# A depthwise convolution of 15 matmuls a channel: three of them get 128 weight columns instead of 64, and the two halves of the input patches are requested together

## What is computed

```
def _L1_conv_ref(x, w_large, w_small, ...):      # x: (1, 384, 192, 192), w_large: 13x13, w_small: 3x3
    out = _bn(_dwconv(x, w_large, 6), g_l, b_l, m_l, v_l) \
        + _bn(_dwconv(x, w_small, 1), g_s, b_s, m_s, v_s) + _bn(x, g_i, b_i, m_i, v_i)
    return out
x = x + _L0_conv_ref(_gn(x), ...)                # layer 0
x = x + _L1_conv_ref(_gn(x), ...)                # layer 1
```

## Time and profile before

| | us |
|---|---|
| median of 3 runs | 2976.05 (2973.62 to 2976.38) |
| the profiled execution | 2976.38 |
| its span, first to last instruction | 2974.7 |
| PE busy in the span | 2670.8 (90%) |
| DVE busy | 2522.6 (85%) |
| ACT busy | 1481.1 (50%) |

### The profile page before, as it was taken

The page is one execution under the profiler, slowest core; times in us unless marked ns, Lnnn a source line. Parts: engine busy times, 40 slices in busy tenths (PEclk is TensorE's granted clock), DMA queues, the critical chain, the costliest instruction groups (busy, mean ns, idle before and its releaser), DMA issues. The chain is left out here.

```text
span 2974.7 us, 50705 instructions
## 1 busy us (share of the span) xinstructions
PE 2670.8 (90%) x17273; PEld 1812.0 (61%) x17273; DVE 2522.6 (85%) x3512; ACT 1481.1 (50%) x1921; POOL 73.9 (2%) x143
## 2 busy tenths in 40 slices
PE   0049999999999999999995999983999999999998
PEld 0036666666666666666663566652777777777776
DVE  7969999999999999999997898984877777777774
ACT  0033445555554554553232667673655555555553
POOL 0010000000000000000000000000000000000000
PEclk9999999999999999999997999995999999999999
DMA  8964112222322322321004999988999999999985
GB/s 333 416 204 144 49 56 93 85 87 84 103 77 93 103 77 87 100 81 48 17 1 152 333 349 346 343 291 177 251 263 261 261 262 261 261 262 260 262 249 169
DMA packets 349112, 546.95 MB, mean 184 GB/s; under 512 B 143392, under 2 KB 254752, under 8 KB 345888
## 3 DMA queue, kind: packets, MB, share of 16 engines
q1 hardware_dynamic: 317504, 436.49, 47.5%
q10 hardware_dynamic: 31456, 108.48, 11.8%
HBM read 364.47 MB, written 180.44 MB: 183 GB/s over the span
## 5 line engine op out<-in xcount | busy, mean ns | idle before, releaser
L781 PE MATMUL qk_qb<-qk_xhi,whi 128*128 128x384 f16 x2592 | 846.4, 327 | 21.0 <-DVE qk_xlo L677 14.3
L781 PE MATMUL qk_qb<-qk_xlo,whi 128*128 128x384 f16 x2592 | 846.2, 326 | 0.0
L781 PE MATMUL qk_qb<-qk_xhi,wlo 128*128 128x384 f16 x2592 | 846.2, 326 | 0.0
L698 DVE SCALAR_TENSOR_TENSOR qk_dw<-qk_pool,qk_wd,qk_dw 128x768 f32<-128x768 f32 (+2 forms) x864 | 836.9, 1009 | 0.1
L685 DVE TENSOR_REDUCE qk_pool<-qk_qb 128x192 f32<-128x768 f32 x432 | 411.9, 954 | 68.7 <-PE qk_qb L781 51.9
L1491 ACT ACTIVATE cv_res<-cv_cb,cv_cst 128x288 f32<-128x288 f32 x384 | 189.8, 502 | 381.5 <-PE cv_cb L1634 331.3
L1628 PE MATMUL cv_cb<-cv_hi,cv_toep 128*128 128x288 f16 x1536 | 346.6, 286 | 35.5 <-DVE cv_lo_last L1559 32.8
L781 PEld LDWEIGHTS qk_qb<-qk_xhi,whi 128*128 128x128 f16 x2592 | 254.0, 98 | 184.2 <-DVE qk_xlo L677 17.5
L781 PEld LDWEIGHTS qk_qb<-qk_xhi,wlo 128*128 128x128 f16 x2592 | 253.9, 98 | 168.4 <-issue 1.2
L1634 PE MATMUL cv_cb<-cv_hi_next,cv_toep 128*128 128x288 f16 x1536 | 356.3, 293 | 0.0
L781 PEld LDWEIGHTS qk_qb<-qk_xlo,whi 128*128 128x128 f16 x2592 | 254.0, 98 | 162.8 <-issue 1.0
(11 more groups left out here) (163 smaller groups left out, 3466.3 us busy)
## 6 DMA issues: line engine op xcount, KB each, us to landing
cv_toep<-toeplitz_scratch SPq DMA_DIRECT2D x384, 256.0 KB, 4.7
patch_scratch<-pr_turned SPq DMA_DIRECT2D x75, 832.0 KB, 9.6
st_x<-in_x SPq DMA_DIRECT2D x24, 2304.0 KB, 17.1
qk_xf<-in_x SPq DMA_DIRECT2D x72, 768.0 KB, 4.3
pr_xb<-in_x SPq DMA_DIRECT2D x24, 2304.0 KB, 10.1
out<-cv_rows ACTq DMA_DIRECT2D x72, 768.0 KB, 5.7
cv_raw<-patch_scratch SPq DMA_DIRECT2D x25, 1300.0 KB, 9.8
cv_raw<-patch_scratch ACTq DMA_DIRECT2D x23, 1300.0 KB, 9.5
```

The source lines that it names most:

```text
L698: V.scalar_tensor_tensor(acc, pool[:, o, r + y:r + y + n, x:x + PW], wd[:, o, k:k + 1], acc, ALU.mult, ALU.add).then_inc(taps_done, 1)
L781: ins = nc.tensor.matmul(qbank[s % NQB][:, h, 0:2 * W], w[:, b, o * P:(o + 1) * P], x[:, par, j // 2, b, at_row:at_row + 2 * W], start=n = ...
```

## The change

Three edits in one stage:
1. `late` gets a second block of 64 columns per channel that GpSimd fills with zeros once. The three matmuls of L1631 take all 128 columns and write all 128 PSUM partitions (zeros are added to the lower 64), with the same 276 moving columns. SP waits for the zeros before the first load of `late`.
2. ACT requests its half of `raw` after the bank copy of channel 0, ahead of `last_high`, instead of after that of channel 5.
3. SP requests its half at its c = 9 instead of c = 8, behind the weights of channel 8, which wait for channel 0 too.

```diff
-        late = sb("late", [P, GRP, ERUN], F16)
+        late = sb("late", [P, GRP, 2, ERUN], F16)
...
-                sp.dma_start(late[:, part_of(q), :],
+                sp.dma_start(late[:, part_of(q), 0, :],
...
-                    if c == GRP // 2 and (inner or g + 2 < NG):
+                    if c == NTOEP + 1 and (inner or g + 2 < NG):
                         address(sp, (g + 2) * (TI * GRP * TJ))
                         sp.wait_ge(edge_done, g * NPC + NPC)
                         start.load_half(sp, g + 2, par, 0)
                     if inner or g < NG:
                         load_taps(g, c)
+                        if at(g, 0) and c == 0:
+                            sp.wait_ge(late_zero, 1)
...
+        @block.gpsimd
+        def _(gp):
+            nc.gpsimd.memset(late[:, :, 1, :], 0.0).then_inc(late_zero, 1)
...
-                    if c == 0:
-                        last_high(g, NPC - 1)
-                    if c == GRP // 2 - 3 and (inner or g + 2 < NG):
+                    if c == 0 and (inner or g + 2 < NG):
                         address(act, (g + 2) * (TI * GRP * TJ))
                         act.wait_ge(edge_done, g * NPC + NPC)
                         start.load_half(act, g + 2, par, 1)
+                    if c == 0:
+                        last_high(g, NPC - 1)
...
-                few = late[:, c, :].rearrange("p (m v) -> p v m", v=2)
+                few = late[:, c].rearrange("p r (m v) -> p v (r m)", v=2)
-                upper = bank[0:HP, 0:NPIX].rearrange("p (j i) -> p j i", j=OJ)[:, :, 0:EI]
...
-                    nc.tensor.matmul(upper, few[:, part], x[:, c, :, 0:EI], start=False, stop=False, skip_group_check=True)
+                    nc.tensor.matmul(whole[:, :, 0:EI], few[:, part], x[:, c, :, 0:EI], start=False, stop=False, skip_group_check=True)
```

More of the change, by code:

```diff
@@ L1368, in stage_depthwise @@
         bbank = [ctx.enter_context(nc.psum_tensor(f"cv_bb{i}", [P, 512], F32)) for i in range(NBB)]
-        cst_in = sem("cst_in")
+        cst_in, late_zero = sem("cst_in"), sem("late_zero")
         toep_in = [sem(f"toep_in{i}") for i in range(NTOEP)]
```

## The result

| | before | after |
|---|---|---|
| median of 4 runs each | 2974.84 (2972.04 to 2976.38) | 2937.91 (2936.08 to 2945.84) |
| span of the profiled execution | 2974.7 | 2934.1 |
| ratio | | 0.988 [0.986, 0.990] |

The account below looks back on a forecast made before the run. PE alone was taken to pace the depthwise stage, with pauses around its 64-column matmuls. The sum 2976.4 - 96.0 + 8.4 + 4.5 = 2893.3, with the median 0.3 lower, gave 2893 us, range 2874 to 2912.

Parts of the forecast that it names:

- 128 columns: The three 64-column matmuls of each depthwise channel, widened: both pauses go, 0.25 us for each of 384 channels, -96.0 us.
- rival D: Pauses around the 64-wide matmuls stay, coming from the change of line or weight tile, not width: 2976 to 2981 us, chance 0.04.
- The zeros: One memset before the first load of `late`: at most 2.4 us, hidden before PE's first matmul, taken as 0.
- The pair: Both halves of `raw` requested together make channel 9's weights late: 0.4 us for 21 groups, +8.4 us (0 to 15.8).
- the bound of 0.75: Most that channel 9's weights could be late per group, if the group's first store takes its turn first: 0.75 us.
- Group 0: SP's half goes out only after DVE's last `norm`, so PE waits once at channel 9: +4.5 us (0 to 6.5).
- The clock: PE's clock might fall after a wait: within the 6.5 us upper bound at group 0's channel 9, no term of its own.
- rival E: Slower: both halves hold up channel 9 in every group, from 4.4 us a group on; 2990 us with 5, chance 0.03.
- DVE and ACT, fits: DVE's 28.62 us fit a 33.4 us group (86%); ACT's bank copy behind the store keeps 1.6 us of slack.
- Rival B: Both halves of `raw` overlap at 406 GB/s, 6.5 us instead of 13, nobody waits: 2880 or 2876 us, chance 0.24.
- Rival C: Transfers pace the depthwise stage: a group takes 34.3 us, saving only 3.0, total 2909 us, chance 0.13.

## Why the prediction was wrong

- **128 columns, -96.0: right in kind, 2.6 us too high.** A group without waits fell from 37.29 to 33.40 us, so 24 of them by 93.4 us; the lower bound was 95. The forecast took 0.25 us a channel and 1.8375 for what is left; 0.243 went. Two readings in it were loose: from the last L1628 to the second L1634 are five steps, not six, and 0.22 us is the idle time of a weight load, of which some 0.12 us reached the matmuls on each side (0.247 for both). The 64-wide kernel with the pair keeps its pauses and the widened one has none, so rival D is refuted.
- **The zeros, 0: right.** The memset took 1.80 us (2.4 estimated) and ended before PE's first matmul by 11 us.
- **The pair, +8.4 (0 to 15.8): the step that failed.** Its mechanism was right, since channel 9's weights were late, behind the pair, in group 0 and in groups 2 to 21. Its size was 2.0 us a group and not 0.4, so 40.2 us outside group 0. Two assumptions failed. The first was "the pair is in at 0.1 + 15.2 = 15.3", taken from a pair with nothing before it. In its place stand 0.6 + 18.3 us: ACT's request went out 0.5 us later, and a store was in flight when the pair was requested; with that store cut to 1% the pair is in after 15.3 us, just the 15.2 assumed, and the wait is gone. The other was the bound of 0.75: I looked for what could come between at the pair's end (the first store) and not at what was ahead at its start. Cutting the first store gained nothing.
- **Group 0, +4.5: 2.7,** of which 0.5 was there before. The right place and wait, oversized by some 2 us.
- **The clock, not in the sum.** I allowed for it in group 0 and under rival E. It fell to 0.50 for some 3.4 us at five places after such waits, and the slower steps cost 13.4 - 1.7 = 11.7 us more than before. So 8.4 + 4.5 of expected loss became 42.9 - 0.5 = 42.4 and 11.7.
- **DVE and ACT, fits: right.** With 128 columns alone DVE is at 84.63 of 100 us and PE is full.
- **Rival B** is refuted in the form in which it stood: the halves go one after the other, at about the rate of one. **Rival C** is refuted by 292 GB/s and a share of 1.01 at full pace. **Rival E** was the true mechanism at half its price: groups 2 to 21 take 2.4 us more than 33.4 each, the clock included, where 4.4 would have made it slower.

What stays open is the last 1.0 us a group of the pair requested three channels later, how the 3.2 us of the store in flight divide between its own transfer and the later request of SP's half, and whether the order in memory has a part in the slow rate of a half.

## What to carry to other kernels

When a transfer is moved forward, ask first what is already in flight at its new place, and take its landing time from a row with the same neighbours. A gain that shortens the work between a request and its use also shortens the cover of every transfer: what was free at 2.085 us a channel cost 2.0 us a group at 1.84. Make the edits of a change one by one; here the first alone was worth 86 us, and the second took back 49.

## What the hardware showed beyond that

A weight load of 128 columns is no longer than one of 64. The line of the `late` matmuls in the changed kernel, loads in min/median/max ns:

```profile
L1636 PEld LDWEIGHTS cv_cb<-cv_hi_last,cv_late x768: 96/98/151, 2065.0 to 2919.8; 128*128 128x128 f16 x192
```

It is 98 ns, against 111 for 64 columns, whose loads ran right ahead of or behind a pause. The Trainium skill ("TensorE: Matmul & The Clock Gate", LDWEIGHTS) has it grow with the columns; these two rows don't agree, and the measurement decides.

The issue of a transfer can itself take long and hold up the queue behind it. Line L1415 between 2100 and 2860, issue times in ns and then landing, in the changed kernel and with 128 columns alone:

```profile
L1415 SPq DMA_DIRECT2D cv_toep<-toeplitz_scratch x342: 534/539/4694, 2101.2 to 2859.7; - x171
...
DMA to landing us min/median/max: 2.7/9.2/18.5
```
```profile
L1415 SPq DMA_DIRECT2D cv_toep<-toeplitz_scratch x360: 534/538/4390, 2101.4 to 2856.8; - x180
...
DMA to landing us min/median/max: 2.8/8.4/17.8
```

Before, the longest such issue was 0.64 us and the median landing 4.8. A transfer of 256 KB, worth 0.65 us at full rate, took up to 18.5 us to land. The second kernel has no early pair, and PE is full in it all the same. The pair only, at 2.085 us a channel, has a longest issue of 1.62 us and landings of 7.4 in the median and 17.0 at most. So late landings come with the faster groups as with the pair. They cost time where PE wants just those weights, and the pair made channel 9's the ones that come last. With the requests for `raw` on 128 partitions the same loads land after 4.5 us in the median and 11.5 at most.
